# Query probabilities transposed in squares of 32 and moved within SBUF instead of by TensorE; double layer weights

## The chip, the core and the metric

The kernel runs on one NeuronCore of a Trainium2 chip. The metric is the device time of one execution in microseconds; lower is better. Five engines run their own instruction streams and meet only at semaphores: TensorE (PE, with its weight loads as PEld), VectorE (DVE), ScalarE (ACT), GpSimd (POOL) and SyncE (SP), which here only issues DMAs.

## What is computed

Eight sequences of 1024 rows by 128 columns go through a modulated layer norm, six layers of linear attention with an MLP, and a final feed-forward block with 4-bit quantisation. The change touches the attention of the six layers alone:

```python
def _linear_attn(q, k, v):
    q = jax.nn.softmax(q, axis=-1)          # over the 16 columns of a head
    k = jax.nn.softmax(k, axis=-2)          # over the 1024 rows
    context = jnp.einsum('bhnd,bhne->bhde', k, v)
    return jnp.einsum('bhnd,bhde->bhne', q, context)
...
for i in range(DEPTH):                      # 6 layers, 8 heads of 16
    xn = _layernorm(x, ln1_w[i], ln1_b[i])
    q, k, v = xn @ wq[i], xn @ wk[i], xn @ wv[i]
    x = _linear_attn(q, k, v) @ wo[i] + bo[i] + x
    xn = _layernorm(x, ln2_w[i], ln2_b[i])
    hdn = xn @ w1[i]                        # 128 -> 512
    hdn = jnp.where(hdn >= 0, hdn, LEAKY_SLOPE * hdn)
    x = hdn @ w2[i] + x
```

## The kernel before

An *item* is one sequence in one layer: `ITEMS` = 6 x 8 = 48, layer by layer, with item `i` working on sequence `i % 8`. The rows of a sequence lie on 128 partitions with T = 8 tiles of 128 columns on each, so one buffer of an item is 128 x 1024 f32. All of x stays in `x_all`.

The order of work is written out by hand. Each engine has a function `emit(v, stages)` that names its pieces of step `v` in order; step `v` works on item `v` ("ahead": norm 1, the key product), `v - 1` (attention), `v - 2` (norm 2), `v - 3` (first MLP product) and `v - 4` and `v - 5` (second MLP product and its addition). An engine never goes past a piece that waits. Buffers are single; each piece waits by semaphore for its inputs and for the readers of what it overwrites.

The pieces of an item that the texts speak of, with their lines in the program before:

- GpSimd: `root1` (L1413 to L1420) and `normalise1` (L1427, eight tiles) make `norm1`; `normalise_q` (L1461) multiplies the exponentials of q by the reciprocal sums and writes `q_prob`; `hidden_low` (L1455) is MLP work.
- TensorE: `turn_norm1` (L369) transposes `norm1` into the PSUM pair S0; `product_k` (L378) and `product_q` (L387) multiply the result, `norm1_t`, by the layer's `wk_s` and `wq_s`; `turn_k` (L393), `product_z` (L400), `turn_z` (L405), `context` (L410) and `context_out` (L415) lead to `ctx_o`, the head-masked context times `wo`; `turn_q` (L420) transposes `q_prob` into S0; `attend` (L427) multiplies `q_prob_t` by `ctx_o` into S1. `turn_norm2` is L437. `first_mlp(f, n)` (L449, L450, L453) and `second_mlp(s, t)` (L466 to L468) are eight pieces each, strewn between the others.
- ScalarE: `first_norm_t` (L628) copies S0 to `norm1_t` with the norm's weights; `exp_k` (L635), `copy_k` (L640), `exp_q` (L645); `copy_q` (L650) copies the turned `q_prob` from S0 to `q_prob_t`.
- VectorE: `max_k` (L950), `max_q` (L955), `shift_q` (L960), `sum_q` (L965), `inverse_q` (L970), `affine_z` (L987), `mask_context` (L993), `bias_context` (L999), `add_attention` (L1005, S1 added to x, signals `x_mid_ready`), the statistics of both norms (L870, L924), `add_mlp` (L1024).
- SyncE: `load_layer(l)` (L256 to L262) loads the four 128 x 128 attention weights of a layer into single buffers, each when its last reader of the layer before is through.

`product_k` of the next item writes S1, from which `add_attention` reads, and so waits for `x_mid_ready`.

## Time and profile before

| | |
|---|---|
| median of 2 runs | 1469.06 us (1468.9 to 1469.21) |
| the profiled execution: time / span | 1468.56 us / 1466.7 us |
| TensorE busy | 1294.5 us, 88% of the span |
| GpSimd busy | 1230.2 us, 84% |
| ScalarE busy | 1064.3 us, 73% |
| VectorE busy | 929.5 us, 63% |
| granted TensorE clock, mean | 0.958 of full |

The span runs from the first to the last instruction of the profiled execution; its time has 1.9 us more around it. Busy shares are averages over parts of different kinds: a start of some 120 us, the items in a fixed rhythm up to about 1140 us, and the feed-forward block after 1230 us. The clock is either at its full 2.4 GHz (1.00) or at 1.2 GHz (0.50); a number between is a mean over a stretch.

### The profile page before, as it was taken

The numbers are of one execution on the slowest core, as the hardware profiler recorded it, in microseconds if no ns is written. First come the engines' busy times: TensorE is split into PE (matmuls) and PEld (weight loads), VectorE is DVE, ScalarE is ACT, GpSimd is POOL, SyncE is SP. The second block draws the span as 40 slices with busy tenths as digits, with TensorE's granted clock in tenths as the row PEclk, the third lists the DMA queues.
The fourth block names the chain that finished last, engine by engine and source line by source line (L and its number), as shares of the span: only waits on it lengthen the run. The fifth ranks groups of instructions, "written<-read, shape, count | busy, mean of one in ns | idle before, by whom it ended". The sixth has DMA issues, their size and how long they took to land.

```text
span 1466.7 us, 31230 instructions
## 1 busy us (share of the span) xinstructions
PE 1294.5 (88%) x11006; PEld 1023.8 (70%) x11006; DVE 929.5 (63%) x2730; ACT 1064.3 (73%) x1716; POOL 1230.2 (84%) x1179
## 2 busy tenths in 40 slices
PE   5577789989999999999999999999999964788896
PEld 2455577878888788888787888887878742355564
DVE  5886645766556565565565665655655415999993
ACT  4376768778887887888878878878888854566663
POOL 4569998888988889889888898898898758999963
PEclk8789989999999999999999999999999986899999
DMA  6000000000000000000000000010000000010000
GB/s 187 15 29 15 2 1 9 2 1 2 2 8 2 2 2 2 9 2 1 2 2 9 1 2 1 2 38 2 1 2 2 2 15 29 15 44 15 29 22 38
DMA packets 12280, 20.64 MB, mean 14 GB/s; under 512 B 1024, under 2 KB 8032, under 8 KB 12128
## 3 DMA queue, kind: packets, MB, share of 16 engines
q1 hardware_dynamic: 12128, 18.65, 3.9%
q8 instruction: 91, 1.49, 0.4%
q14 instruction: 61, 0.50, 0.1%
HBM read 14.45 MB, written 4.19 MB: 13 GB/s over the span
## 4 chain that ended last, share of the span: by engine, by line
POOL 57%; issue 26%; PE 10%; DVE 4%; ACT 2%; POOLq 0%; DMA 0%; DVEq 0%; ACTq 0%
POOL hidden L1455 25%; POOL arena L1427 9%; POOL arena L1447 7%; POOL arena L1461 6%; PE ring_pair L565 1%; PE pair L587 1%; POOL arena L1554 1%; PE ring_pair L559 1%; POOL rstd L1386 1%; PE mlp L574 1%; POOL x_all L1405 1%; POOL x_all L1515 1%; POOL mod_in L1529 1%; POOL f_rstd L1386 1%; POOL ve L1434 1%
## 5 line engine op out<-in xcount | busy, mean ns | idle before, releaser
L1455 POOL TENSOR_TENSOR hidden<-hidden 128x2048 f16<-128x2048 f32 x94 | 384.4, 4089 | 14.7 <-ACT hidden L690 14.7
L683 ACT ACTIVATE hidden<-ring_pair 128x512 f32<-128x512 f32 x384 | 218.3, 591 | 64.0 <-PE ring_pair L453 57.7
L690 ACT ACTIVATE hidden<-hidden 128x2048 f16<-128x2048 f32 x96 | 183.0, 1907 | 58.1 <-PE mlp L468 58.0
L1461 POOL TENSOR_TENSOR arena<-arena,q_rec 128x1024 f32<-128x1024 f32 x48 | 97.1, 2022 | 104.8 <-DVE q_rec L970 104.8
L1386 POOL TENSOR_TENSOR rstd<-ve,minus_half 128x8 f32<-128x8 f32 x104 | 174.4, 1677 | 10.3 <-DVE ve L890 6.9
L870 DVE BATCH_NORM_STATS2 bn<-x_all 128x6 f32<-128x128 f32 x832 | 171.2, 278 | 6.1 <-DVE x_all L1005 1.4
L1427 POOL TENSOR_SCALAR arena<-x_all,rstd,nmr 128x128 f32<-128x128 f32 x384 | 167.2, 452 | 5.0
L466 PE MATMUL pair_mlp<-halves,hidden 128*128 128x128 f16 x768 | 141.9, 223 | 20.8 <-issue 14.3
L659 ACT ACTIVATE arena<-x_all,nmr,rstd 128x128 f32<-128x128 f32 x384 | 157.0, 485 | 0.0
L449 PE MATMUL ring_pair<-arena,halves 128*128 128x512 f16 x384 | 147.0, 383 | 7.4 <-ACT hidden L683 7.0
L453 PE MATMUL ring_pair<-arena,halves 128*128 128x512 f16 x384 | 146.5, 382 | 2.8 <-POOL arena L1447 2.8
L450 PE MATMUL ring_pair<-arena,halves 128*128 128x512 f16 x384 | 146.8, 382 | 0.0
L466 PE MATMUL mlp<-halves,hidden 128*128 128x128 f16 x768 | 137.2, 221 | 8.2 <-issue 8.2
L467 PE MATMUL pair_mlp<-halves,hidden 128*128 128x128 f16 x768 | 141.9, 223 | 0.0
L468 PE MATMUL pair_mlp<-halves,hidden 128*128 128x128 f16 x768 | 141.9, 223 | 0.0
L467 PE MATMUL mlp<-halves,hidden 128*128 128x128 f16 x768 | 137.2, 221 | 0.0
L468 PE MATMUL mlp<-halves,hidden 128*128 128x128 f16 x768 | 137.2, 220 | 0.0
L1447 POOL TENSOR_TENSOR arena<-arena 128x1024 f16<-128x1024 f32 x48 | 102.2, 2130 | 31.4 <-ACT arena L674 31.4
L1005 DVE TENSOR_TENSOR x_all<-pair_mlp,x_all 128x1024 f32<-128x1024 f32 x48 | 58.8, 1225 | 102.5 <-PE pair_mlp L427 102.5
L950 DVE TENSOR_REDUCE cols<-pair_mlp 128x1 f32<-128x1024 f32 x48 | 58.8, 1225 | 89.4 <-PE pair_mlp L378 89.4
L628 ACT ACTIVATE arena<-pair,ln_cols 128x1024 f32<-128x1024 f32 x48 | 57.8, 1204 | 66.8 <-PE pair L369 66.8
L427 PEld LDWEIGHTS pair_mlp<-small,arena 128*128 128x128 f32 x768 | 91.0, 195 | 18.3 <-DVE small L999 18.3
(202 smaller groups left out, 3585.5 us busy)
## 6 DMA issues: line engine op xcount, KB each, us to landing
x_in<-in_L_attn_x SPq DMA_DIRECT2D x16, 512.0 KB, 3.5
out_x<-x_all SPq DMA_DIRECT2D x8, 512.0 KB, 2.6
hidden<-in_L_attn_w SPq DMA_DIRECT2D x1, 1536.0 KB, 8.5
hidden<-in_L_attn_w SPq DMA_DIRECT2D x6, 256.0 KB, 8.1
arena<-in_L_wmod SPq DMA_DIRECT2D x1, 384.0 KB, 2.9
bo_rows<-in_L_attn_bo SPq DMA_DIRECT2D x1, 384.0 KB, 5.5
wk_s<-in_L_attn_wk SPq DMA_DIRECT2D x6, 64.0 KB, 1.8
wq_s<-in_L_attn_wq SPq DMA_DIRECT2D x6, 64.0 KB, 1.7
```

The costliest lines, as they stand in the source:

```text
L466: nc.tensor.matmul(o, rows_hi, hi, start=(c == 0), stop=False)
L467: nc.tensor.matmul(o, rows_hi, lo, start=False, stop=False)
L468: last = nc.tensor.matmul(o, rows_lo, hi, start=False, stop=(c == HC - 1))
L659: last = act.activation(tile(norm2, t), x_all[:, bass.ds((i % B) * W + t * D, D)], ACT.Identity, scale=rstd2[:, t:t + 1], bias=nmr2[:, t:t ...
L683: act.activation(hidden_t[:, c * W + h * HALF:c * W + (h + 1) * HALF], ring[n % 2], ACT.Prelu, scale=HIDDEN_DOWN, alpha=LEAKY).then_inc(hi ...
L690: act.activation(half_rows(hidden_hi, h), half_rows(hidden_t, h), ACT.Copy).then_inc(hidden_hi_ready, 1)
L870: last = nc.vector.bn_stats(bn[:, 6 * t:6 * t + 6], src(t))
L1386: return pool.tensor_tensor(rstd[:, 0:tiles], ve[:, 0:tiles], minus_half[:, 0:tiles], ALU.pow).then_inc(rstd_ready, 1)
L1427: last = pool.tensor_scalar(tile(norm1, t), x_all[:, bass.ds((i % B) * W + t * D, D)], rstd1[:, t:t + 1], nmr1[:, t:t + 1], ALU.mult, ALU.add)
L1447: pool.tensor_tensor(norm2_lo, norm2_t, norm2_hi, ALU.subtract).then_inc(norm2_lo_ready, 1)
L1455: pool.tensor_tensor(half_rows(hidden_lo, h), half_rows(hidden_t, h), half_rows(hidden_hi, h), ALU.subtract).then_inc(hidden_lo_ready, 1)
L1461: pool.tensor_tensor(q_prob.rearrange("p (g d) -> p g d", d=DH), q_exp.rearrange("p (g d) -> p g d", d=DH), q_rec[:, :].unsqueeze(2).to_br ...
```

## The change

`turn_q` on TensorE and `copy_q` on ScalarE go. In their place VectorE's `block_q` transposes `q_prob` in squares of 32 x 32 within each group of 32 partitions into a new buffer `q_blocks`, and SyncE moves the squares to their partitions in `q_prob_t` with 16 transfers for each item (`move_q`), 32 partitions x 1 KB each, written in two pieces of 512 bytes for each partition. So that the squares fall into place, `first_norm_t` writes the columns of `norm1_t` in another order, in two instructions, and `product_k` reads them back in the old order; q therefore has its rows in a permuted order until `attend`, which gives the old order again. `attend` waits for all 16 transfers, and its place on TensorE moves from ahead of `turn_norm1` to directly ahead of `product_k`; `second_mlp` 7 moves ahead of it. `turn_norm1` waits for `q_shifted` instead of `q_prob_t_ready`. The four weight buffers are doubled, so that a layer's load waits for the layer before the last.

```diff
@@ -90,7 +90,10 @@
         identity = sb("identity", P)
         head_mask = sb("head_mask", D)
         minus_half = sb("minus_half", T)
-        wk_s, wq_s, wv_s, wo_s = (sb(n, D) for n in ("wk_s", "wq_s", "wv_s", "wo_s"))
+        wk_s, wq_s, wv_s, wo_s = (sb(n, 2 * D) for n in ("wk_s", "wq_s", "wv_s", "wo_s"))
+        q_blocks = sb("q_blocks", W)[:, :]
+        QB = P // 32
+        MOVES = QB * QB
...
@@ -252,14 +255,25 @@
             sp.dma_start(bo_rows[:, :], bo_src.to_broadcast((P, DEPTH * D))).then_inc(bo_loaded, 16)
             def load_layer(l):
 
-                after(sp, k_done, l * B)
-                sp.dma_start(wk_s[:, :], wk[bass.ds(l, 1)].rearrange("l f o -> f (l o)")).then_inc(wk_ready, 16)
...
+                c = l % 2 * D
+                after(sp, k_done, (l - 1) * B)
+                sp.dma_start(wk_s[:, c:c + D], wk[l:l + 1].rearrange("l f o -> f (l o)")).then_inc(wk_ready, 16)
...
+            def move_q(i):
+
+                sp.wait_ge(q_blocks_ready, i + 1)
+                after(sp, attn_done, i)
+                for j in range(QB):
+                    to = q_prob_t[32 * j:32 * (j + 1), :].rearrange("r (a n k) -> r a n k", a=T // QB, n=QB)
+                    for n in range(QB):
+                        rows = q_blocks[32 * n:32 * (n + 1), j * T * 32:(j + 1) * T * 32].rearrange("r (a k) -> r a k", a=T // QB)
+                        sp.dma_start(to[:, :, n], rows).then_inc(q_prob_t_ready, 16)
 
             def load_x(b):
                 return sp.dma_start(x_in[:, bass.ds((b % 2) * W, W)], x_rows[bass.ds(b, 1)].rearrange("b p k -> p (b k)"))
@@ -277,14 +291,17 @@
                 sp.wait_ge(x_rest_loaded, 16 * (b - 2))
                 sp.wait_ge(front_hat_ready, b - 2)
                 load_x(b).then_inc(x_rest_loaded, 16)
-            for l in range(1, DEPTH):
-                load_layer(l)
-
-
-            sp.wait_ge(front_ready, B)
-            load_x(0).then_inc(x_back_loaded, 16)
-            sp.wait_ge(x_back_loaded, 16)
-            load_x(1).then_inc(x_back_loaded, 16)
+                move_q(b - 3)
+            load_layer(1)
+            for i in range(B - 3, ITEMS):
+                move_q(i)
+                if i == B:
+                    sp.wait_ge(front_ready, B)
+                    load_x(0).then_inc(x_back_loaded, 16)
+                    sp.wait_ge(x_back_loaded, 16)
+                    load_x(1).then_inc(x_back_loaded, 16)
+                if i % B == B - 1 and i // B + 2 < DEPTH:
+                    load_layer(i // B + 2)
 
 
             def store(b):
@@ -364,7 +381,7 @@
 
             def turn_norm1(i):
                 pe.wait_ge(norm1_ready, i + 1)
-                after(pe, q_prob_t_ready, i)
+                after(pe, q_shifted, i)
                 for t in range(T):
                     last = nc.tensor.transpose(tile(S0, t), tile(norm1, t), identity[:, :])
                 last.then_inc(t1_done, 1)
@@ -373,18 +390,20 @@
 
                 pe.wait_ge(norm1_t_ready, i + 1)
                 pe.wait_ge(wk_ready, 16 * (i // B + 1))
+                w = wk_s[:, i // B % 2 * D:i // B % 2 * D + D]
                 after(pe, x_mid_ready, i)
                 for h in range(2):
-                    last = nc.tensor.matmul(S1[:, h * HALF:(h + 1) * HALF], wk_s[:, :],
-                                            norm1_t[:, h * HALF:(h + 1) * HALF], start=True, stop=True)
+                    last = nc.tensor.matmul(S1[:, h * HALF:(h + 1) * HALF], w,
+                                            norm1_t[:, h * HALF:(h + 1) * HALF].rearrange("p (i n c) -> p n i c", i=QB, n=QB), start=True, stop=True)
                 last.then_inc(k_done, 1)
 
...
@@ -407,22 +426,18 @@
...
-
-            def turn_q(i):
-                pe.wait_ge(q_prob_ready, i + 1)
-                for t in range(T):
-                    last = nc.tensor.transpose(tile(S0, t), tile(q_prob, t), identity[:, :])
-                last.then_inc(q_turned, 1)
+                w = wo_s[:, i // B % 2 * D:i // B % 2 * D + D]
+                nc.tensor.matmul(S1[:, HALF:HALF + D], ctx_t, w, start=True, stop=True).then_inc(ctx_o_done, 1)
 
             def attend(i):
                 pe.wait_ge(ctx_o_ready, i + 1)
-                pe.wait_ge(q_prob_t_ready, i + 1)
+                pe.wait_ge(q_prob_t_ready, 16 * MOVES * (i + 1))
                 for t in range(T):
                     last = nc.tensor.matmul(tile(S1, t), tile(q_prob_t, t), ctx_o, start=True, stop=True)
                 last.then_inc(attn_done, 1)
@@ -492,17 +507,16 @@
                 if second: second_mlp(s, 4)
                 if first: first_mlp(f, 5)
                 if attention: context(a)
-                if attention: turn_q(a)
                 if first: first_mlp(f, 6)
                 if attention: context_out(a)
                 if first: first_mlp(f, 7)
-                if attention: attend(a)
                 if ahead: turn_norm1(v)
                 if norm: turn_norm2(n)
                 if second: second_mlp(s, 5)
                 if second: second_mlp(s, 6)
+                if second: second_mlp(s, 7)
+                if attention: attend(a)
                 if ahead: product_k(v)
-                if second: second_mlp(s, 7)
 
             phases(emit, pe)
             drain(emit, 0)
@@ -625,8 +639,11 @@
 
                 act.wait_ge(t1_done, i + 1)
                 after(act, q_done, i)
-                act.activation(norm1_t, S0[:, :], ACT.Identity, scale=layer_col(LN1W, i // B),
-                               bias=layer_col(LN1B, i // B)).then_inc(norm1_t_ready, 1)
+                for h in range(2):
+                    last = act.activation(norm1_t[:, h * HALF:(h + 1) * HALF].rearrange("p (i n c) -> p n i c", i=QB, n=QB),
+                                          S0[:, h * HALF:(h + 1) * HALF].rearrange("p (n i c) -> p n i c", i=QB, n=QB),
+                                          ACT.Identity, scale=layer_col(LN1W, i // B), bias=layer_col(LN1B, i // B))
+                last.then_inc(norm1_t_ready, 1)
 
             def exp_k(i):
                 act.wait_ge(k_max_ready, i + 1)
@@ -643,11 +660,6 @@
                 act.wait_ge(q_shifted, i + 1)
                 after(act, q_prob_ready, i)
                 act.activation(q_exp, q_shift, ACT.Exp).then_inc(q_exp_ready, 1)
-
-            def copy_q(i):
-                act.wait_ge(q_turned, i + 1)
-                after(act, attn_done, i)
-                act.activation(q_prob_t, S0[:, :], ACT.Copy).then_inc(q_prob_t_ready, 1)
 
             def normalise2(i, h):
 
...
@@ -968,6 +979,12 @@
                 dve.wait_ge(q_sum_ready, i + 1)
                 after(dve, q_prob_ready, i)
                 nc.vector.reciprocal(q_rec[:, :], q_sum[:, :]).then_inc(q_rec_ready, 1)
+
+            def block_q(i):
+                dve.wait_ge(q_prob_ready, i + 1)
+                after(dve, q_prob_t_ready, 16 * MOVES * i)
+                nc.vector.transpose(q_blocks.rearrange("p (j t c) -> p t j c", j=QB, t=T),
+                                    q_prob.rearrange("p (t j c) -> p t j c", j=QB, t=T)).then_inc(q_blocks_ready, 1)
 
             def inverse_k(i):
                 dve.wait_ge(k_exp_t_ready, i + 1)
@@ -1134,6 +1151,7 @@
                 if isinstance(v, int) and 4 <= v < 8:
                     prepare_gates((v - 4) // 2, v % 2 * 2 + 1)
                 if attention: affine_z(a)
+                if attention: block_q(a)
                 if isinstance(v, int) and v == 1:
                     prepare_scales()
                 if isinstance(v, int) and v == 0:
@@ -1457,7 +1475,7 @@
 
             def normalise_q(i):
                 pool.wait_ge(q_rec_ready, i + 1)
-                after(pool, q_turned, i)
+                after(pool, q_blocks_ready, i)
                 pool.tensor_tensor(q_prob.rearrange("p (g d) -> p g d", d=DH), q_exp.rearrange("p (g d) -> p g d", d=DH),
                                    q_rec[:, :].unsqueeze(2).to_broadcast((P, GROUPS, DH)), ALU.mult).then_inc(q_prob_ready, 1)
 ```

How the change moves instructions, at three places (names as in the program; `arena` holds the item buffers, `pair` is S0, `pair_mlp` is S1 and the first MLP bank, `halves` and `hidden` belong to the MLP; in brackets the semaphores waited for).

TensorE before, from `context_out` to `turn_norm2` in a step of full rhythm:

```order
L415 MATMUL pair_mlp<-wo_s,small 128x128 [waits wo_ready,ctx_t_ready]
L449 MATMUL ring_pair<-arena,halves 128x512 [waits hidden_copied,weights_ready]
L450 MATMUL ring_pair<-arena,halves 128x512
L453 MATMUL ring_pair<-arena,halves 128x512 [waits norm2_lo_ready,weights_ready]
L427 MATMUL pair_mlp<-small,arena 128x128 [waits q_prob_t_ready,ctx_o_ready]
L427 MATMUL pair_mlp<-small,arena 128x128 x7
L369 MATMUL pair<-identity,arena 128x128 [waits q_prob_t_ready,norm1_ready]
L369 MATMUL pair<-identity,arena 128x128 x7
L437 MATMUL ring_pair<-identity,arena 128x128 [waits hidden_copied,norm2_ready]
L437 MATMUL ring_pair<-identity,arena 128x128 x7
```

TensorE in the change, the same stretch (L436 is `context_out`, L386 `turn_norm1`, L452 `turn_norm2`):

```order
L436 MATMUL pair_mlp<-wo_s,small 128x128 [waits wo_ready,ctx_t_ready]
L464 MATMUL ring_pair<-arena,halves 128x512 [waits hidden_copied,weights_ready]
L465 MATMUL ring_pair<-arena,halves 128x512
L468 MATMUL ring_pair<-arena,halves 128x512 [waits norm2_lo_ready,weights_ready]
L386 MATMUL pair<-identity,arena 128x128 [waits q_shifted,norm1_ready]
L386 MATMUL pair<-identity,arena 128x128 x7
L452 MATMUL ring_pair<-identity,arena 128x128 [waits hidden_copied,norm2_ready]
L452 MATMUL ring_pair<-identity,arena 128x128 x7
```

`attend` has left this place, and the eight transposes of `turn_q`, which stood between `context` and the `first_mlp` piece ahead of `context_out`, are gone.

TensorE in the change, the end of the step and the start of the next (L483 ends `second_mlp` 7, L442 is `attend`, L396 `product_k`, L481 starts `second_mlp` 0):

```order
L483 MATMUL mlp<-halves,hidden 128x128
L442 MATMUL pair_mlp<-small,arena 128x128 [waits q_prob_t_ready,ctx_o_ready]
L442 MATMUL pair_mlp<-small,arena 128x128 x7
L396 MATMUL pair_mlp<-arena,wk_s 128x512 [waits x_mid_ready,wk_ready,norm1_t_ready]
L396 MATMUL pair_mlp<-arena,wk_s 128x512
L481 MATMUL pair_mlp<-halves,hidden 128x128 [waits x_ready,hidden_lo_ready,weights_ready]
```

`attend` now stands directly ahead of `product_k`, which waits for `x_mid_ready`; before, `turn_norm1`, `turn_norm2` and `second_mlp` 5 and 6 stood between them.

VectorE before, from `inverse_q` to `add_attention`:

```order
L970 RECIPROCAL q_rec<-q_sum 128x64 [waits q_prob_ready,q_sum_ready]
L981 TENSOR_SCALAR small<-pair_mlp,cols 128x128 [waits z_turned,k_rec_ready,z_done]
L987 TENSOR_SCALAR small<-pair_mlp,ln_cols 128x128 [waits ctx_done,z_turned]
L993 TENSOR_TENSOR small<-pair_mlp,head_mask 128x128 [waits ctx_o_done,ctx_done]
L1024 SCALAR_TENSOR_TENSOR x_all<-pair_mlp,mlp_up,x_all 128x512 [waits mlp_done]
L999 SCALAR_TENSOR_TENSOR small<-bo_rows,pair_mlp 128x128 [waits attn_done,ctx_o_done]
L1005 TENSOR_TENSOR x_all<-pair_mlp,x_all 128x1024 [waits attn_done]
```

VectorE in the change, the same stretch:

```order
L981 RECIPROCAL q_rec<-q_sum 128x64 [waits q_prob_ready,q_sum_ready]
L998 TENSOR_SCALAR small<-pair_mlp,cols 128x128 [waits z_turned,k_rec_ready,z_done]
L1004 TENSOR_SCALAR small<-pair_mlp,ln_cols 128x128 [waits ctx_done,z_turned]
L986 STREAM_TRANSPOSE q_blocks<-arena 128x8x4x32 [waits q_prob_t_ready,q_prob_ready]
L1010 TENSOR_TENSOR small<-pair_mlp,head_mask 128x128 [waits ctx_o_done,ctx_done]
L1041 SCALAR_TENSOR_TENSOR x_all<-pair_mlp,mlp_up,x_all 128x512 [waits mlp_done]
L1016 SCALAR_TENSOR_TENSOR small<-bo_rows,pair_mlp 128x128 [waits attn_done,ctx_o_done]
L1022 TENSOR_TENSOR x_all<-pair_mlp,x_all 128x1024 [waits attn_done]
```

`block_q` (L986) has come in between `affine_z` and `mask_context`; it waits for `q_prob` of GpSimd and for the transfers of the item before.

## Rows read from the trace of the kernel before

**Rows 1.** Busy time by stage (columns: stretch, us, engines, TensorE clock, DMA share, GB/s).
```profile
120.00:237.00 117.00, 94.85 (x822) 78.66 (x823) 71.18 (x215) 80.45 (x128) 106.31 (x93) 0.93 0.02 6
700.00:1140.00 440.00, 429.61 (x4073) 355.07 (x4072) 262.27 (x878) 360.13 (x513) 387.47 (x395) 1.00 0.02 5
```

**Rows 2.** Timeline of TensorE, one item (start, length, line, count, idle before).
```profile
708.22 1.95 PE L427 MATMUL pair_mlp<-small,arena 128*128 128x128 f32 x16
710.69 1.10 PE L369 MATMUL pair<-identity,arena 128*128 128x128 f32 x8 [0.52 <-POOL arena L1427]
...
713.84 1.94 PE L378 MATMUL pair_mlp<-arena,wk_s 128*128 128x512 f32 x4
715.61 0.22 PE L466 MATMUL mlp<-halves,hidden 128*128 128x128 f16 x1
...
716.95 2.00 PE L387 MATMUL pair<-wq_s,arena 128*128 128x128 f32 x16
718.79 0.22 PE L466 MATMUL pair_mlp<-halves,hidden 128*128 128x128 f16 x1
...
728.35 1.04 PE L420 MATMUL pair<-identity,arena 128*128 128x128 f32 x8
729.22 0.38 PE L449 MATMUL ring_pair<-arena,halves 128*128 128x512 f16 x1
...
733.20 1.09 PE L369 MATMUL pair<-identity,arena 128*128 128x128 f32 x8 [0.52 <-POOL arena L1427]
```

**Rows 3.** Timeline of GpSimd, same item.
```profile
725.47 1.93 POOL L1461 TENSOR_TENSOR arena<-arena,q_rec 128x1024 f32<-128x1024 f32 x1 [1.80 <-DVE q_rec L970]
...
729.70 3.45 POOL L1427 TENSOR_SCALAR arena<-x_all,rstd,nmr 128x128 f32<-128x128 f32 x8
```

**Rows 4.** Timeline of VectorE, same item.
```profile
710.21 1.23 DVE L1005 TENSOR_TENSOR x_all<-pair_mlp,x_all 128x1024 f32<-128x1024 f32 x1 [2.14 <-PE pair_mlp L427]
...
713.28 0.64 DVE L924 BATCH_NORM_AGGREGATE mv<-bn 128x2 f32<-128x6 f32 x8
...
718.99 1.22 DVE L955 TENSOR_REDUCE q_max<-pair 128x64 f32<-128x1024 f32 x1 [1.29 <-PE pair L387]
...
728.55 0.29 DVE L993 TENSOR_TENSOR small<-pair_mlp,head_mask 128x128 f32<-128x128 f32 x1 [1.77 <-PE pair_mlp L410]
```

**Rows 5.** DMA issues of the page, and SyncE's timeline.
```profile
wk_s<-in_L_attn_wk SPq DMA_DIRECT2D x6, 64.0 KB, 1.8
...
14.22 0.43 SPq L256 DMA_DIRECT2D wk_s<-in_L_attn_wk  x1
14.70 0.43 SPq L258 DMA_DIRECT2D wq_s<-in_L_attn_wq  x1
...
603.23 0.33 SPq L256 DMA_DIRECT2D wk_s<-in_L_attn_wk  x1
```

**Rows 6.** Timeline of TensorE, three gaps (last column: idle before).
```profile
154.65 0.22 PE L466 MATMUL pair_mlp<-halves,hidden 128*128 128x128 f16 x1 [3.15 <-issue]
...
183.38 0.22 PE L466 MATMUL pair_mlp<-halves,hidden 128*128 128x128 f16 x1 [3.17 <-issue]
...
212.26 0.26 PE L466 MATMUL pair_mlp<-halves,hidden 128*128 128x128 f16 x1 [3.15 <-issue]
```

**Rows 7.** Busy time and clock of stretches after the three gaps.
```profile
155.00:160.00 5.00, 5.00 (x52) 4.31 (x49) 4.78 (x9) 3.73 (x9) 4.92 (x6) 1.00 0.01 3
184.00:187.00 3.00, 3.00 (x18) 3.00 (x16) 0.00 (x0) 2.39 (x7) 3.00 (x4) 0.51 0.00 0
212.00:218.00 6.00, 5.74 (x38) 5.71 (x39) 0.75 (x1) 0.21 (x2) 5.92 (x7) 0.50 0.00 0
```

**Rows 8.** Timelines of GpSimd and VectorE at 1212 us.
```profile
1211.47 1.27 POOL L1509 TENSOR_TENSOR mod_in<-x_all,mod_out 128x512 f32<-128x512 f32 x1
1212.88 3.13 POOL L1515 TENSOR_TENSOR x_all<-mod_in,x_in 128x512 f32<-128x512 f32 x1
...
1211.99 2.89 DVE L1017 TENSOR_TENSOR hidden<-hidden 128x2048 f16<-128x2048 f32 x1
```

More of the change, by code:

```diff
@@ L385, in product_q @@
                 pe.wait_ge(wq_ready, 16 * (i // B + 1))
+                w = wq_s[:, i // B % 2 * D:i // B % 2 * D + D]
                 for t in range(T):
-                    last = nc.tensor.matmul(tile(S0, t), tile(norm1_t, t), wq_s[:, :], start=True, stop=True)
+                    last = nc.tensor.matmul(tile(S0, t), tile(norm1_t, t), w, start=True, stop=True)
                 last.then_inc(q_done, 1)
@@ L724, in emit @@
                     prepare_weights(1)
-                if attention: copy_q(a)
                 if first: hidden_high(f, 0)
```

20 lines of the change are left out of this document (10 added, 10 removed).

## Prediction

> **What bounds the kernel now.** I first read the busy time by stage [rows 1]. From 237 us on, TensorE is busy 429.6 of 440 us at the full clock (1.00) and GpSimd 387.5; between 120 and 237 us GpSimd has 106.3 of 117. Shares don't say which of the two sets the pace, so I then followed one item through the timelines of the three engines [rows 2 to 4]. `turn_norm1` (L369) starts at 710.69 and again at 733.20, so an item takes 22.51 us. The only idle time of TensorE in it is the 0.52 us ahead of L369, ended by GpSimd's L1427. The ring that closes there is:
> - `turn_norm1`, `turn_norm2`, `second_mlp` 5 and 6, from L369 to L378: 713.84 - 710.69 = 3.15
> - `product_k`, to 715.61: 1.77
> - `second_mlp` 7 and 0, to L387 at 716.95: 1.34, so 0.67 each
> - `product_q`, until VectorE's `max_q` (L955) starts at 718.99: 2.04
> - `max_q`, shift, exp, sum and reciprocal, until GpSimd's `normalise_q` (L1461) starts at 725.47: 6.48
> - `normalise_q`, `root1`, `normalise1`, until the next L369 at 733.20: 7.73
>
> The sum is 22.51, the whole period: a closed ring through TensorE, VectorE, ScalarE and GpSimd. `attend` (L427) is not in it; it fills the time in which TensorE would otherwise wait for `normalise1`. Anything put into the ring costs its full length for every item; anything taken out of TensorE elsewhere gives nothing.
>
> **The edits, one by one.** *`turn_q` and `copy_q` go.* L420 to the next L449 is 729.22 - 728.35 = 0.87 us [rows 2]. It lies between `product_q` and `turn_norm1`, where TensorE waits for GpSimd anyway; ScalarE is not late for anybody in the ring. Gain 0.
>
> *Weights double.* A load is issued in 0.33 us and lands in 1.8 [rows 5], against almost a period between the last use and the next. It was hidden, so doubling gains 0. Loads of the next layer now queue on SyncE behind the moves, with a layer to spare.
>
> *`attend` behind `second_mlp` 7, directly ahead of `product_k`.* This is the edit that counts. `product_k` waits for `x_mid_ready`, that is for `add_attention` (L1005), which waits for `attend`. Before, eight turns of norm1, eight of norm2 and two pieces of `second_mlp` covered that wait. Now the ring holds `attend` until the addition starts, 710.21 - 708.22 = 1.99 [rows 2, 4], and the addition, 1.23, with 0.05 to hand over (GpSimd's last row ends at 729.70 + 3.45 = 733.15, L369 starts at 733.20) [rows 3]. The new ring is 3.15 + 0.67 + 1.99 + 1.28 + 1.77 + 0.67 + 2.04 + 6.48 + 7.73 = 25.78, or 3.27 more. VectorE's other work doesn't lengthen it: the statistics after the addition end 713.28 + 0.64 - 710.21 = 3.71 us after its start, `max_k` (1.2) and `add_mlp` (0.7) then end about 5.6 after it, and `product_q` ends 1.28 + 1.77 + 0.67 + 2.04 = 5.76 after it. It is just covered. 40 of the 48 items lie in the stretch from 237 us on (901 us to the last `turn_norm1`): 40 x 3.27 = 131 us.
>
> *`block_q`.* The trace has no DVE transpose. The nearest rows are VectorE's passes over 128x1024 f32, 1.22 to 1.23 us [rows 4]; I take 1.2. Below it lies at best half of that, above it 2.5. It runs at 727.4, when `q_prob` is there (725.47 + 1.93), in VectorE's 1.77 us of idle time ahead of `mask_context` (L993). Queued behind it are `mask_context` and with it `context_out` on TensorE, which would be up to 1 us late at the upper end. TensorE has that time before `turn_norm1`, so it costs 0. The Trainium skill (VectorE: DVE Perf Modes, "The three transpose paths") gives 311 ns for a 128x128 bf16 transpose in squares of 32. Eight such would be an estimate of 2.5 us where my rows say 1.2; by it `q_blocks` would come 1.3 us later, and if nothing else delayed `attend`, the sum would be some 45 us higher. No row here shows which.
>
> *16 transfers on SyncE for each item.* The nearest rows are the layer loads: 0.33 us alone, 0.47 from start to start in a row of them (14.22, 14.70), 1.8 from issue to landing. I take 0.42 between issues. `q_prob` at 727.40, transpose and hand-over 1.3, 15 x 0.42 = 6.3, landing 1.8: 9.4 us. `attend` would run at 733.20 + 3.15 + 0.67 = 737.02, 9.6 us after `q_prob`. The transfers are just hidden; at 0.47 they are 0.55 us late. If a short transfer took 0.6 us to issue they would be 2.5 us late, 100 us in all.
>
> *TensorE's new idle time.* From the end of `product_q`'s issue (718.79) to `turn_norm1` stay 14.41 us, and TensorE's work in it was 11.94 (to 730.73, one period after 708.22), now 11.07 without `turn_q`. A gap of 3.3 us arises in every item ahead of `turn_norm1`, and a second one of 1.3 behind `attend`. The trace has three gaps of that size, 3.15 to 3.17 us [rows 6]. After the first the clock stayed at 1.00. Around the second it fell to its lower level, 1.2 GHz (0.51 from 184 to 187), and around the third from 212 to 218 (0.50) [rows 7]. TensorE was busy all but 0.26 us of these 9, so the losses were 0, 1.5 and 2.9 us, mean 1.5. What follows the gap here is the ring's own TensorE work, so the loss is paid in full: 40 x 1.5 = 60 us. It also delays `attend`, which hides late transfers.
>
> *First items, layer change, tail.* Between 120 and 237 us GpSimd sets the pace and TensorE has gaps of 3.15 us, just what the longer TensorE part needs: 0. The first three items have no MLP work to cover the transfers: 9.4 us instead of the 3.3 from `q_prob` (727.40) to `attend` (730.73), 6 us for each of three, of which I take 10 in all. For the last item once 4. In three items VectorE has work for the FFN weights between `max_k` and `max_q`, whose 1.29 us of slack [rows 4] is used up: 4.
>
> **Sum.** It is made against the profiled execution's 1468.56 us (median 1469.06, so 0.5 apart). 1468.6 + 131 + 10 + 4 + 4 = 1618 without the clock, and + 60 = 1678.
>
> **Rivals.** *A. Ring and clock*, 1678: the sum above. For it: two of three gaps of this size. *B. Ring alone*, 1618: the clock holds, as after the first gap. *C. Transfers late*: `attend` waits for SyncE. For it: 9.4 against 9.6 is no margin, and the gap before `attend` then adds to the idle time; with 0.55 to 2.5 us each it gives 1640 to 1720 on top of the ring, and with the clock up to 1780. Against it: a move has 64 pieces of 512 bytes, a layer load 128. *D. Not slower than before*: TensorE's own issue sets the pace, and what counts is that it loses 0.87 us of work for each item; 1468.6 - 40 x 0.87 = 1434. It decides if `normalise1` came before TensorE was through and `add_attention` cost nothing on TensorE; the 98% busy share speaks for it, against it the 0.52 us ahead of L369, ended by GpSimd each time, and the closed sum of 22.51. *E. GpSimd held up by `block_q`*: the one row of GpSimd beside a long VectorE instruction with two inputs from SBUF took 3.13 us, its neighbours of the same size 1.27 [rows 8]. If the transpose did that to `root1` and `normalise1`, the ring would grow by up to its 1.2 us, 48 in all: 1726 with the clock. The Trainium skill (SBUF — State Buffer, "Who interferes with whom") says that VectorE and GpSimd share one port pair, which a VectorE instruction takes with two SBUF inputs or in a two-port mode; the row agrees for two inputs, and the transpose has one.
>
> **How the numbers follow.** A 0.5, B 0.2, C 0.17, E 0.08, D 0.05. The likeliest gives 1678; I say 1675. The range takes in B less some microseconds and most of C: 1600 to 1765. A difference of about 2% (1440 to 1498) is what a measurement of this kernel tells from no change. D lies just at its lower edge: faster 0.03, same 0.03, slower 0.94.
>
> **What would show it.** The profile after should have: a period near 27 us from 240 us on; idle time of `product_k` ended by VectorE's addition, about 1.3 us each; idle time ahead of `turn_norm1` ended by GpSimd, about 3 us; clock below 1.00 in that stretch (B: at 1.00 and a period of 25.8); `attend` waiting for no DMA (C: it does); a transpose of 1.2 us. I am wrong if the period stays under 24 us, which would mean that the ring isn't closed as I read it, or if SyncE's 16 issues take far over 7 us.

## The result, and the profile after

The changed kernel takes 1836.5 us (median of 2 runs, 1827.74 to 1845.26) against 1469.06: a ratio of 1.250 with a 95% interval of 1.225 to 1.276, slower. The prediction said slower, but 1675 us with a range that ended at 1765. The profiled execution took 1845.26 us (span 1843.5), 377 more than that of before.

From the page of the changed kernel: busy time, the granted clock by slices, the groups of section 5 that answer to [rows 2 to 4], and the transfers.

```profile
PE 1373.4 (74%) x10622; PEld 1066.0 (58%) x10622; DVE 981.7 (53%) x2778; ACT 1033.1 (56%) x1716; POOL 1226.3 (67%) x1179
...
PEclk8689989889898989989899898989898888779999
...
L1022 DVE TENSOR_TENSOR x_all<-pair_mlp,x_all 128x1024 f32<-128x1024 f32 x48 | 58.8, 1225 | 633.5 <-PE pair_mlp L442 633.5
...
L1479 POOL TENSOR_TENSOR arena<-arena,q_rec 128x1024 f32<-128x1024 f32 x48 | 97.1, 2022 | 166.2 <-DVE q_rec L981 166.2
...
L442 PE MATMUL pair_mlp<-small,arena 128*128 128x128 f32 x768 | 116.0, 314 | 111.1 <-DMA arena<-q_blocks 111.1
...
L386 PE MATMUL pair<-identity,arena 128*128 128x128 f32 x384 | 77.2, 367 | 151.0 <-POOL arena L1445 151.0
...
L396 PE MATMUL pair_mlp<-arena,wk_s 128*128 128x512 f32 x192 | 109.2, 697 | 70.8 <-DVE x_all L1022 66.2
...
arena<-q_blocks SPq DMA_DIRECT2D x768, 32.0 KB, 1.9
```

Three waits are new in kind or size. TensorE's `product_k` (L396) now waits for VectorE's addition (L1022), 66.2 us in all; `turn_norm1` (L386) waits 151.0 us for GpSimd's `normalise1`; and `attend` (L442) waits 111.1 us for the transfers. All three are what the prediction had as signs, the third as the sign of its rival C. How they come together is seen in one item (its 16 issues hold one long one, as 22 of the 48 do): TensorE first, without the pieces of the MLP.

```profile
883.14 1.09 PE L386 MATMUL pair<-identity,arena 128*128 128x128 f32 x8 [3.16 <-POOL arena L1445]
...
890.27 2.02 PE L442 MATMUL pair_mlp<-small,arena 128*128 128x128 f32 x16 [1.51 <-DMA arena<-q_blocks]
893.70 1.96 PE L396 MATMUL pair_mlp<-arena,wk_s 128*128 128x512 f32 x4 [1.41 <-DVE x_all L1022]
...
896.16 2.00 PE L406 MATMUL pair<-wq_s,arena 128*128 128x128 f32 x16
...
912.42 1.97 PE L386 MATMUL pair<-identity,arena 128*128 128x128 f32 x8 [3.16 <-POOL arena L1445]
...
920.59 2.02 PE L442 MATMUL pair_mlp<-small,arena 128*128 128x128 f32 x16 [1.34 <-DMA arena<-q_blocks]
```

VectorE in the same item (`block_q` is L986), then GpSimd (`normalise_q` is L1479, `normalise1` L1445):

```profile
892.33 1.23 DVE L1022 TENSOR_TENSOR x_all<-pair_mlp,x_all 128x1024 f32<-128x1024 f32 x1 [12.67 <-PE pair_mlp L442]
...
898.21 1.22 DVE L966 TENSOR_REDUCE q_max<-pair 128x64 f32<-128x1024 f32 x1 [0.39 <-PE pair L406]
...
904.08 0.52 DVE L981 RECIPROCAL q_rec<-q_sum 128x64 f32<-128x64 f32 x1
...
906.65 1.25 DVE L986 STREAM_TRANSPOSE q_blocks<-arena 128x1024 f32<-128x1024 f32 x1 [0.66 <-POOL arena L1479]
907.82 0.25 DVE L1010 TENSOR_TENSOR small<-pair_mlp,head_mask 128x128 f32<-128x128 f32 x1
```

```profile
904.68 1.93 POOL L1479 TENSOR_TENSOR arena<-arena,q_rec 128x1024 f32<-128x1024 f32 x1 [2.27 <-DVE q_rec L981]
...
906.89 1.64 POOL L1404 TENSOR_TENSOR rstd<-ve,minus_half 128x8 f32<-128x8 f32 x1
...
908.91 3.45 POOL L1445 TENSOR_SCALAR arena<-x_all,rstd,nmr 128x128 f32<-128x128 f32 x8
```

And SyncE's 16 issues of the same item (the view of one line: shortest, median and longest issue in ns, the first and last start, then the time to landing):

```profile
L276 SPq DMA_DIRECT2D arena<-q_blocks x16: 586/596/1643, 907.9 to 918.5; - x16
...
DMA to landing us min/median/max: 1.9/1.9/3.1
```

Read as a ring, as [rows 2 to 4] were: `attend` at 890.27 until the addition starts 2.06, to `product_k` 1.37, to `product_q` 2.46, to `max_q` 2.05, to `normalise_q` 6.47, to `block_q` 1.97, to the first issue (907.92) 1.27, and from there to the next `attend` at 920.59 12.67. The sum is 30.32, the period of this item. The ring that closes no longer goes through `normalise1` and `turn_norm1`; it goes through SyncE: `attend` waits for the transfers in all 48 items. The 16 starts lie 0.64 us apart, here one pair 1.69, so that the last comes 10.6 us after the first. In most items without a long issue it comes 9.6 after, `attend` starts 12.9 us after `q_prob` is there, and the period is 29.3 if the clock stays up. The granted clock is below full as well:

```profile
400.00:1300.00 900.00, 699.76 (x5946) 565.76 (x5945) 424.81 (x1356) 524.92 (x765) 590.35 (x597) 0.92 0.08 20
```

The low clock costs time only where it falls between `attend` and `product_q`. That is so in 10 of the last 36 items: from `attend` to the next `normalise_q` they take 15.6 to 18.2 us, the other 26 take 14.41. In the rest the wait for the transfers covers it, as at 912.42, where `turn_norm1` takes 1.97 us instead of 1.09 and `attend` waits all the same.

### The profile page after: what moved, and what is told of

Its sections match the earlier page's. It is cut to its first block, busy times and chain, and to the rows that moved or that the text cites. A ratio compares the mean times of both kernels' runs of the same rounds, so it can differ in the third digit from the quotient of the medians.

```text
span 1843.5 us, 31325 instructions
## 1 busy us (share of the span) xinstructions
PE 1373.4 (74%) x10622; PEld 1066.0 (58%) x10622; DVE 981.7 (53%) x2778; ACT 1033.1 (56%) x1716; POOL 1226.3 (67%) x1179
## 4 chain that ended last, share of the span: by engine, by line
issue 38%; POOL 35%; PE 14%; ACT 5%; DVE 4%; SPq 3%; DMA 1%; POOLq 0%; DVEq 0%; ACTq 0%
POOL hidden L1473 10%; POOL arena L1445 7%; POOL arena L1479 5%; POOL arena L1465 5%; PE pair L386 3%; ACT arena L686 3%; SPq L276 3%; PE ring_pair L452 3%; PE pair L601 1%; PE ring_pair L579 1%; PE ring_pair L573 1%; POOL arena L1572 1%; PE pair_mlp L442 1%; PE mlp L588 1%; DVE bn L881 1%
## 5 line engine op out<-in xcount | busy, mean ns | idle before, releaser
L1022 DVE TENSOR_TENSOR x_all<-pair_mlp,x_all 128x1024 f32<-128x1024 f32 x48 | 58.8, 1225 | 633.5 <-PE pair_mlp L442 633.5
L652 ACT ACTIVATE arena<-pair_mlp,cols 128x1024 f32<-128x1024 f32 x48 | 53.5, 1114 | 363.5 <-DVE cols L961 363.5
L1479 POOL TENSOR_TENSOR arena<-arena,q_rec 128x1024 f32<-128x1024 f32 x48 | 97.1, 2022 | 166.2 <-DVE q_rec L981 166.2
L1452 POOL TENSOR_TENSOR ve<-mv,eps_cols 128x8 f32<-128x8 f32 x48 | 10.4, 218 | 286.0 <-DVE mv L935 286.0
L442 PE MATMUL pair_mlp<-small,arena 128*128 128x128 f32 x768 | 116.0, 314 | 111.1 <-DMA arena<-q_blocks 111.1
L386 PE MATMUL pair<-identity,arena 128*128 128x128 f32 x384 | 77.2, 367 | 151.0 <-POOL arena L1445 151.0
L1404 POOL TENSOR_TENSOR rstd<-ve,minus_half 128x8 f32<-128x8 f32 x104 | 171.4, 1648 | 12.2 <-DVE ve L901 8.7
L442 PEld LDWEIGHTS pair_mlp<-small,arena 128*128 128x128 f32 x768 | 106.9, 223 | 118.7 <-issue 118.7
L1445 POOL TENSOR_SCALAR arena<-x_all,rstd,nmr 128x128 f32<-128x128 f32 x384 | 167.1, 452 | 5.0
L464 PE MATMUL ring_pair<-arena,halves 128*128 128x512 f16 x384 | 147.5, 384 | 29.0 <-ACT hidden L695 28.7
L481 PE MATMUL mlp<-halves,hidden 128*128 128x128 f16 x768 | 157.3, 240 | 9.6 <-issue 9.6
L396 PE MATMUL pair_mlp<-arena,wk_s 128*128 128x512 f32 x192 | 109.2, 697 | 70.8 <-DVE x_all L1022 66.2
L386 PEld LDWEIGHTS pair<-identity,arena 128*128 128x128 f32 x384 | 60.7, 187 | 174.2 <-POOL arena L1445 174.2
L482 PE MATMUL mlp<-halves,hidden 128*128 128x128 f16 x768 | 155.9, 239 | 0.0
L483 PE MATMUL mlp<-halves,hidden 128*128 128x128 f16 x768 | 154.6, 237 | 0.0
L643 ACT ACTIVATE arena<-pair,ln_cols 128x512 f32<-128x512 f32 x96 | 69.4, 773 | 150.1 <-PE pair L386 150.1
```

The source lines that it names most:

```text
L386: last = nc.tensor.transpose(tile(S0, t), tile(norm1, t), identity[:, :])
L442: last = nc.tensor.matmul(tile(S1, t), tile(q_prob_t, t), ctx_o, start=True, stop=True)
L481: nc.tensor.matmul(o, rows_hi, hi, start=(c == 0), stop=False)
L1404: return pool.tensor_tensor(rstd[:, 0:tiles], ve[:, 0:tiles], minus_half[:, 0:tiles], ALU.pow).then_inc(rstd_ready, 1)
L1445: last = pool.tensor_scalar(tile(norm1, t), x_all[:, bass.ds((i % B) * W + t * D, D)], rstd1[:, t:t + 1], nmr1[:, t:t + 1], ALU.mult, ALU.add)
L1479: pool.tensor_tensor(q_prob.rearrange("p (g d) -> p g d", d=DH), q_exp.rearrange("p (g d) -> p g d", d=DH), q_rec[:, :].unsqueeze(2).to_br ...
```

## The experiments

All are timed beside the kernel before (its medians 1468.4 to 1469.5 us); e5 ran once, for its profile alone. To compare stretches, the starts of `add_attention` were listed from VectorE's timeline in each profile. "First 12" is the start in the 12th item, "steady" the time from there to the 48th, 36 periods (us):

| kernel | first 12 | steady | one period |
|---|---|---|---|
| before | 350.0 | 810.4 | 22.51 |
| e6, order, gap filled | 395.7 | 935.7 | 25.97 |
| e1, order alone | 401.6 | 983.5 | 26.0 or 27.6 |
| e3, change, two queues | 414.6 | 983.3 | 27.3 or 27.6 |
| after | 442.9 | 1096.4 | 29.3 to 32.5, mean 30.5 |

**The order alone.** The kernel before with only `attend` and `second_mlp` 7 in the places that the change gives them; TensorE still turns q.

```diff
-                if attention: attend(a)
...
-                if ahead: product_k(v)
                 if second: second_mlp(s, 7)
+                if attention: attend(a)
+                if ahead: product_k(v)
```

> The kernel before with one edit: attend stands behind second_mlp 7, directly ahead of product_k; turn_q and copy_q stay and nothing is transferred. Theory 1 (the ring with attend and the addition in it costs 3.3 us for each item, and the transfers the rest of what was measured): a period of 25.8 us from 240 us on, 1469 + 131 = about 1600 us, up to 1660 if the 2.4 us gap ahead of turn_norm1 lowers the clock. Theory 2 (the place of attend costs nothing, all of the loss is the transfers): 1469 us. Theory 3 (the clock is the larger part): 1700 us or more, with clock rows at 0.50 in most items.

1692.9 us (1691.1 to 1693.8), ratio 1.152 [1.150, 1.154]. Two lines of order cost 223 of the 367 us. Of 36 periods 29 are 27.6, six 26.0 and the last 26.8. In TensorE's timeline the wait for the addition is the whole of the predicted one, and the clock of the stretch is below full:

```profile
703.40 1.96 PE L378 MATMUL pair_mlp<-arena,wk_s 128*128 128x512 f32 x4 [1.41 <-DVE x_all L1005]
...
722.16 1.13 PE L369 MATMUL pair<-identity,arena 128*128 128x128 f32 x8 [2.35 <-POOL arena L1427]
```

```profile
400.00:1300.00 900.00, 776.27 (x6879) 641.26 (x6878) 440.45 (x1485) 611.61 (x859) 657.43 (x660) 0.95 0.01 4
```

**The same, with the gap filled.** In e1, sixteen identity transposes that nothing reads, ahead of `turn_norm1`. The wait for S0 to be free moves ahead of them.

```diff
+                after(pe, q_prob_t_ready, i)
+                if i > 1:
+                    for t in range(16):
+                        nc.tensor.transpose(tile(S0, t % T), identity[:, :], identity[:, :])
                 pe.wait_ge(norm1_ready, i + 1)
-                after(pe, q_prob_t_ready, i)
```

> e1_order_only with 16 transposes of the identity ahead of each turn_norm1, whose result is overwritten: work without use, 1.8 us, in the gap in which TensorE waits for normalise1. If the 1.5 us by which the long periods of e1 (27.6) stand above the short ones (26.0) are the clock falling in that gap, the clock stays at 1.00, all periods are 26.0 and the time falls by about 36 x 1.25 = 45 us to 1645, although more work is done. If the clock isn't the cause, the time stays at 1693 or rises.

```profile
400.00:1300.00 900.00, 831.80 (x7801) 693.10 (x7801) 463.00 (x1558) 639.24 (x907) 691.49 (x697) 1.00 0.01 4
```

1638.2 us (1635.9 to 1640.0), ratio 1.116 [1.113, 1.118]: more work, 55 us less time. The clock is 1.00 throughout and every period but the last 26.0. So of e1's excess the ring is 26.0 - 22.51 = 3.5 us for each item and the clock the rest, 983.5 - 935.7 = 48 us in the steady stretch, where the prediction's 1.5 for each item gives 54.

**`attend` behind two fewer pieces.** In e1, `attend` moves ahead of the last pieces, so that `second_mlp` 6 and 7 run while the addition does.

```diff
+                if attention: attend(a)
                 if second: second_mlp(s, 6)
                 if second: second_mlp(s, 7)
-                if attention: attend(a)
                 if ahead: product_k(v)
```

> e1_order_only with attend behind second_mlp 5 instead of 7, so that pieces 6 and 7 (1.34 us) cover the addition of attention ahead of product_k. By the ring it falls from 26.0 to 24.7 us, about 50 us less than e1: 1640 us. If the wait for the addition were covered by something else, 1693 us.

1609.0 us (1606.5 to 1609.8), ratio 1.095 [1.094, 1.097]. The periods are 24.6 (expected 24.7) and 26.3; the latter, where the clock fell, come in 15 of 36 items, where e1 has 29 long ones; 14 x 1.65 = 23 us of the 31 by which the time lies below what was expected. The wait for the addition is a matter of place: 1.35 us of cover gives 1.4 back.

**The shape of the transfers.** The changed kernel, with the columns of `q_prob_t` laid out so that a transfer writes 1 KB on a partition in one piece instead of two; `attend` takes its tiles in the matching order.

```diff
-                        rows = q_blocks[32 * n:32 * (n + 1), j * T * 32:(j + 1) * T * 32].rearrange("r (a k) -> r a k", a=T // QB)
-                        sp.dma_start(to[:, :, n], rows).then_inc(q_prob_t_ready, 16)
+                        rows = q_blocks[32 * n:32 * (n + 1), j * T * 32:(j + 1) * T * 32]
+                        to = q_prob_t[32 * j:32 * (j + 1), n * T * 32:(n + 1) * T * 32]
+                        sp.dma_start(to, rows).then_inc(q_prob_t_ready, 16)
```

> The change with one edit: the columns of q_prob_t are laid out so that each transfer writes 1 KB in one piece for each partition instead of two of 512 bytes; still 16 transfers of 32 KB. If the 0.64 us between two issues comes from the second dimension or the number of pieces (64 against 32), issues come every 0.33 to 0.47 us, attend no longer waits for them, and the time falls to about 1680 us. If an issue costs 0.6 us whatever the pieces, the time stays at 1836 us.

1826.1 us (1815.6 to 1834.7), ratio 1.240 [1.234, 1.247]; the median issue is 591 ns instead of 597, and 22 of the 48 bursts have one long issue, as many as before. The pieces are not the cause.

**What an issue costs.** The kernel before, with six groups of 16 issues on SyncE behind everything else, into parts of x that nobody reads any more. The first group:

```diff
+            for n in range(16):
+                sp.dma_start(x_all[32:64, n * 256:(n + 1) * 256], bo_rows[0:32, 0:256]).then_inc(priced, 16)
+            sp.wait_ge(priced, 16 * 16)
```

> The kernel before, with six groups of 16 transfers on SyncE behind the last store, each group after the landing of the one before, no engine else at work: within SBUF 32 partitions x 1 KB in one piece, then in two pieces of 512 bytes, then 128 partitions x 1 KB, then from HBM 32 partitions x 1 KB, then from HBM 128 x 1 KB, then within SBUF 16 partitions x 1 KB. They overwrite x_all when it is stored, so the output is that of before. It prices the issue. If the price hangs on the direction, the HBM groups come every 0.33 to 0.47 us and those within SBUF every 0.6; if it hangs on a queue already being full, all come alike and the first of a group is the shortest; if on the pieces, the second group is slower than the first. Total about 60 us above before.

One execution, 1536.6 us. SyncE's timeline at the end of the span (the length is that of 16 issues together):

```profile
1466.68 10.11 SPq L307 DMA_DIRECT2D x_all<-bo_rows  x16
1478.07 10.26 SPq L310 DMA_DIRECT2D x_all<-bo_rows  x16
1489.62 10.19 SPq L314 DMA_DIRECT2D x_all<-bo_rows  x16
1501.31 7.31 SPq L317 DMA_DIRECT2D x_all<-in_L_attn_x  x16
1509.91 7.55 SPq L320 DMA_DIRECT2D x_all<-in_L_attn_x  x16
1523.00 10.08 SPq L323 DMA_DIRECT2D x_all<-bo_rows  x16
```

From 32 partitions of SBUF in one piece (L307), in two pieces (L310), from 128 partitions (L314) and from 16 (L323) the 16 take 10.1 to 10.3 us, 0.63 to 0.64 each; from HBM (L317 with 32 partitions, L320 with 128) 7.3 and 7.6, 0.46 to 0.47 each. None of the 96 issues is a long one. The layer loads of [rows 5] come from HBM. They were the wrong row for a move within SBUF, and no row of before shows one. It is not the source alone: the eight stores of the kernel before (`out_x`, from SBUF to HBM, one at a time) are issued in 0.33 to 0.35 us. What makes an issue within SBUF dearer is open.

**Two queues.** The changed kernel, with ScalarE issuing half of the transfers, behind `copy_hidden` 7.

```diff
-                for j in range(QB):
+                for j in range(QB // 2):
...
+            def move_q(i):
+                act.wait_ge(q_blocks_ready, i + 1)
+                after(act, attn_done, i)
+                for j in range(QB // 2, QB):
...
+                        act.dma_start(to[:, :, n], rows).then_inc(q_prob_t_ready, 16)
...
+                if attention: move_q(a)
```

> The change with one edit: 8 of the 16 transfers are issued by ScalarE behind its last copy_hidden piece, 8 by SyncE. Theory 1 (the issues set the period): the last transfer lands 5 us earlier, attend waits only for its place behind turn_norm1, period near 25.8 us plus what the clock takes, 1620 to 1700 us. Theory 3 (clock): no more than 30 us below 1836. If it is the DMA engines and not the issuing that takes the time, also no change.

1704.0 us (1703.7 to 1705.5), ratio 1.160 [1.158, 1.161]: 132 us less than the change, and within 11 of the order alone. `attend` waits for no transfer in the steady stretch, and that stretch is as long as e1's (983.3 and 983.5). The 13 us between the two profiles are all in the first 12 items. That the two stretches are equal to 0.2 us is chance in part: e1 loses some 1.6 us to the clock in 29 of 36 items, e3 1.3 in nearly every one. But the rest of the ring is the same in both, 14.39 us from `attend` to the next `normalise_q` and 7.77 from there to `turn_norm1`. So once the transfers come in time, transposing on VectorE gives back none of what the order costs, and costs nothing beside it. The issuing was the limit, and not the DMA engines: the same 16 transfers, issued by two engines side by side (ScalarE's lie 0.66 us apart), have landed 9.2 to 10.6 us after `q_prob`, and `attend` comes after 11.0.

**Two queues, gap filled.** e3, with 24 such transposes ahead of `turn_norm1` (the diff is that of e6 with 24 for 16 and `q_shifted` for `q_prob_t_ready`).

> The kernel e3 (the change, with half of its transfers issued by ScalarE) with 24 identity transposes of 128x128 that nothing reads, ahead of turn_norm1, in the gap in which TensorE waits 3.2 us for normalise1. They add work and compute nothing. Theory: e3's period of 27.3 us is the ring of 26.0 plus what the lower clock costs, so that with the gap filled the clock stays at 1.00, the period is 26.0 and the time 1704 - 1.3 x 36 = about 1655 us. Rival: the 27.3 is something of ScalarE's or SP's issuing, and the period stays 27.3 or grows with the added work: 1704 us or more.

1667.0 us (1665.8 to 1667.6), ratio 1.135 [1.134, 1.137]. The clock is at 1.00 from 400 to 1300 us and 37 us come back of the 47 that the clock alone would give. The periods are 26.0 to 29.6, mean 26.6, since `attend` now waits for transfers again in 20 of 34 items from 400 to 1300 us, 14.2 us in all:

```profile
PE pair_mlp L445 <- DMA arena<-q_blocks: 14.2, 20, 1.9
```

This is mostly `attend` coming earlier. At the full clock it is ready 9.64 us after `q_prob`, where in e3 it was 11.0, and the last transfer has landed after 9.3 to 11.6 us, in only two of the 36 items after more than 11.0. The lower clock of e3 had covered the rest. Both theories had a part: the clock is the larger one.

**`attend` where it was.** The changed kernel, with `attend` back ahead of `turn_norm1` and `second_mlp` 7 behind `product_k`.

```diff
+                if attention: attend(a)
                 if ahead: turn_norm1(v)
...
-                if second: second_mlp(s, 7)
-                if attention: attend(a)
                 if ahead: product_k(v)
+                if second: second_mlp(s, 7)
```

> The change with attend back at its old place ahead of turn_norm1 and second_mlp 7 back behind product_k; transpose and transfers stay. Theory 1: attend waits for the transfers 13.9 us after q_prob and turn_norm1 now queues behind it, ring 1.97 + 1.27 + 12.67 + 1.74 + 3.15 + 1.77 + 1.34 + 2.04 + 6.47 = 32.4 us, so about 1900 us, slower than the change. If the new place of attend were the main cost, it would fall below 1700 us.

1998.9 us (1997.3 to 1999.5), ratio 1.360 [1.358, 1.362], period 34.1. The transfers then stand between `q_prob` and `turn_norm1`; `attend` waits 269.4 us for them in 26 items from 400 to 1300 us. The late place was thus the better one for 16 transfers, though it costs 3.5 us. The period is 1.7 above what was expected, and TensorE's timeline shows by what: behind a wait of 10.3 us `attend` takes 3.55 to `turn_norm1` at the lower clock instead of the 1.74 of the sum, and from there to `product_k` it is 4.05 instead of 3.15; against that, this item has no long issue, 1.05 less.

**Is TensorE's work worth anything?** The kernel before, with `turn_q` doing one transpose instead of eight.

```diff
-                for t in range(T):
+                for t in range(1):
                     last = nc.tensor.transpose(tile(S0, t), tile(q_prob, t), identity[:, :])
```

> The kernel before, with turn_q cut from eight transposes to one: copy_q still copies all of S0, and attend still reads all of q_prob_t, so seven eighths of the query probabilities are left untransposed. It takes 7/8 x 0.87 = 0.76 us of TensorE's work out of every item. Theory (a ring through GpSimd sets the period, and turn_q lies in TensorE's waiting time): the period stays 22.51 us and the time 1469 us. Rival D of the prediction (TensorE's own issue sets the pace): 0.76 x 40 = 30 us less, 1438 us.

1466.8 us (1465.1 to 1469.7), ratio 0.999 [0.998, 1.000]; the period stays 22.5 and TensorE waits longer instead, 38.3 us at L369 from 400 to 1100 us where it had waited 16.1. This is the change's gain on TensorE, paid out alone: nothing.

**Taking GpSimd out of the ring.** The ring of [rows 2 to 4] says what would pay: `normalise_q` stands on GpSimd ahead of `root1` and `normalise1`, 1.93 us of it. In the kernel before, it goes to VectorE.

```diff
+            def normalise_q(i):
+                dve.wait_ge(q_rec_ready, i + 1)
+                after(dve, q_turned, i)
+                nc.vector.tensor_tensor(heads(q_prob), heads(q_exp), q_rec[:, :].unsqueeze(2).to_broadcast((P, GROUPS, DH)),
+                                        ALU.mult).then_inc(q_prob_ready, 1)
...
+                if attention: normalise_q(a)
...
-                if attention: normalise_q(v - 1)
```

First directly behind `inverse_q`:

> The kernel before with one edit: normalise_q runs on VectorE behind inverse_q instead of on GpSimd. If the ring is as read, GpSimd's part of it falls by 1.93 us and root1 no longer waits for the reciprocal; the ring falls below TensorE's own 21.8 us of work, which then sets the pace: 0.7 us less for each of 40 items, about 1440 us, faster than both. If GpSimd or VectorE are held up at their shared port by it, the time is 1469 or more.

1472.4 us (1468.2 to 1474.6), ratio 1.002 [1.001, 1.004], period 22.74. TensorE's waits for GpSimd are gone, but one of another kind has come, since `scale_z` now stands behind a pass of 1.2 us:

```profile
PE pair_mlp L405 <- DVE small L987: 23.4, 31, 0.8
```

Then the same function, its call moved two pieces on, behind `affine_z`:

> The kernel before, with normalise_q moved to VectorE as in the run e7, but written behind affine_z instead of behind inverse_q. In e7 GpSimd was out of the ring and the period stayed 22.74 us, since TensorE then waited 0.8 us at turn_z for scale_z, which stood behind normalise_q. Theory (that wait was all that held e7): the period falls to TensorE's own 21.8 to 21.9 us, 0.6 x 40 = 25 us less than before, 1445 us. Rival (something of VectorE's own row, not the place of one instruction, sets the period with normalise_q there): 1469 us or more, with another wait on VectorE in each item.

1421.4 us (1421.2 to 1426.5), ratio 0.969 [0.967, 0.970], faster than both kernels. From 400 to 1100 us TensorE waits for nobody:

```profile
400.00:1100.00 700.00, 700.00 (x6720) 582.29 (x6719) 469.15 (x1482) 591.12 (x835) 601.78 (x610) 1.00 0.02 5
```

The steady stretch takes 783.8 us, 26.6 less than before (21.78 a period, as expected); another 18.4 come in the first 12 items (331.6), which I had not counted. GpSimd had set the pace in part of them and has 1.9 us less to do in each; that this is the cause was not tested.

**And `turn_q` once more,** with the same cut as in e11, now where TensorE sets the pace:

> The same cut of turn_q (one transpose instead of eight, seven eighths of the query probabilities left untransposed) in the kernel e9, in whose steady stretch TensorE waits for nobody. Theory: now TensorE's own work sets the period of 21.78 us, so the 0.76 us come off it in every item, 0.76 x 40 = 30 us, period 21.0 and 1391 us. Rival (something else stands right behind at 21.8): less than half of that, over 1406 us.

1395.6 us (1395.2 to 1400.8), ratio 0.950 [0.948, 0.952]; the period is 21.16. The cut that gave nothing before is worth 26 us here, 0.61 for each item of the 0.76 expected.

## Why the prediction was wrong

**The step that failed** is the fifth of the edits, "I take 0.42 between issues", and with it "The transfers are just hidden". The issues lie 0.64 us apart. With that the same sum, `block_q` and hand-over 1.3, issues 9.6, landing 1.9, gives 12.8 us from `q_prob` to `attend`, and 12.9 is measured in the items without a long issue; in the item shown, with one of 1.64, it is 920.59 - (904.68 + 1.93) = 13.98. Against that stand the 9.6 us of cover, which were right (9.64 in e10), so `attend` is late by 3.3 us in every item. The mechanism was named (rival C, and "if SyncE's 16 issues take far over 7 us"), but it was held for unlikely because the 0.42 came from loads out of HBM; even its upper value, 0.6 for an issue and 100 us in all, lies below what the transfers cost.

In the steady stretch of the changed kernel, from `attend` to `attend`, the ring of the new order takes 36 x (25.97 - 22.51) = 125 us more than before, the transfers 36 x (29.27 - 25.97) = 119, long issues 18, and the clock, where it falls in the ring, 23. That is 285 of 286. Without the late transfers the clock costs more: against e1, which pays 48 for it, the changed kernel is 1096.4 - 983.5 = 113 slower. In the first 12 items the transfers cost 442.9 - 401.6 = 41, where I had 10 for them.

**A second, smaller one:** "Between 120 and 237 us ... 0", and the 4 us for the FFN weights. Before any transfer is late (e1 against before) the first 12 items cost 401.6 - 350.0 = 52 us; my terms there, four periods with the clock and 4 us for the FFN weights, make 23. With the gap filled (e6) 46 remain. By periods these are 15 us in the first four, nothing in the fifth and sixth, as I had expected of all, 6 in the seventh and the eleventh, and 25 in the eighth to tenth, in which VectorE has its work for the FFN weights. Of these 25 the longer ring is 10. In each of the three, one instruction of that work takes 4.0 to 5.2 us (two of them below), 3.8 to 3.9 more than in before, 11.6 in all; that these make the remaining 15 is argued.

**What held.** The closed ring of 22.51 and the new one: 25.78 forecast, 26.0 in e1, e6 and e10. The wait of `product_k` for the addition, 1.3 forecast, 1.41 measured. The gap ahead of `turn_norm1`, 3.3 and 3.16. The transpose, 1.2 and 1.25 (L986), no sum of eight times 311 ns. Nothing for `turn_q` (e11), and nothing for `copy_q`, so far as the equal rings of e1 and e3 show it. Rival D fell with e11, and e12 shows the point from which it decides: once no ring through GpSimd stands in front. The doubled weights were not tried alone, but the last 36 periods of before are 22.50 to 22.52 us through four changes of layer, so a load that could be hidden better isn't there. Rival E fell: in 46 of the 48 items `block_q` runs beside `root1`, whose long instruction takes 1.64 us (L1404) as in before; `normalise1` takes 3.45 as in [rows 3], but it starts after `block_q` has ended and so says nothing on it.

**The clock** was the right mechanism, shown by e6, and its size fits the order alone: 54 us forecast for 36 items, 48 measured in the steady stretch. A mean over three gaps (0, 1.5 and 2.9 us) could not promise that, so the closeness is in part luck, and the prediction took gaps of 3.2 us for it where that of e1 is 2.35. In the changed kernel the clock costs 23, since the waits for transfers take its place.

The sum by differences between kernels, for the profiled executions: 1468.6, ring 125, clock 48, first 12 items 52 + 41, transfers 113, makes 1847.6; the tail gives 2 back, against 1845.3.

## What to carry to other kernels

Before moving work off an engine, find out whether its time is on the ring that closes each period: 0.76 us of TensorE's 22.51 were worth nothing until the 1.93 us of GpSimd behind them were moved, and then 0.61, and one instruction's place on VectorE then decided between 1472 and 1421 us. An engine swap that needs many small transfers is priced by issue time times count on the issuing engine, from a row of the same kind (from SBUF to SBUF, not from HBM), and both the length of the burst and the distance to its reader belong in the sum. A step directly ahead of another that waits for its consumer costs the consumer's full time; two short pieces between them give it back.

## What the runs showed of the hardware

- A DMA issue on SyncE takes 0.63 to 0.64 us from SBUF to SBUF and 0.46 to 0.47 from HBM to SBUF in a row of 16, with 32 or 128 partitions alike, and within SBUF with 16 partitions or two pieces as well (e5). Alone, a load from HBM took 0.33 and a store from SBUF to HBM 0.33 to 0.35 (before).
- In 22 of the 48 bursts of the changed kernel one issue took 1.1 to 1.8 us, all others at most 0.78. The trace's DMA records show an instruction load at each of them: a packet of 16 KB on queue q8 starts within 0.32 us of the long issue in all 22, and no other packet of q8 falls in a burst. In e2 it is again 22 of 22, and in e5 no such packet and no long issue falls in the six rows. The 18 packets of 8 KB on queue q14 that meet a burst lengthen none. Why the one kind holds an issue up is open. In the item shown, DMA from 913.4 to 913.9 us:

```profile
q1 hardware_dynamic: 73, 0.03, 25.4%
q8 instruction: 1, 0.02, 16.7%
```

- TensorE fell to its lower clock behind gaps of 2.35 us in 29 of 36 items (e1) and of 3.2 us in nearly every item (e3); useless transposes in the gap kept it at 2.4 GHz and saved 55 us (e6) and 37 us (e10).
- VectorE's TENSOR_SCALAR on 128x70 f32 took 4.04 us in e1, where in before it took 0.20, and that on 128x1120 4.66 instead of 0.78. Each started beside GpSimd's `hidden_low`; the first ended with it, the second 0.6 us after it. VectorE's and GpSimd's timelines of e1:

```profile
281.60 4.04 DVE L1181 TENSOR_SCALAR f_w_scale<-f_w_max 128x70 f32<-128x70 f32 x1
...
313.43 4.66 DVE L1189 TENSOR_SCALAR f_w_m<-f_w 128x1120 int32<-128x1120 int32 x1
```

```profile
281.51 4.08 POOL L1455 TENSOR_TENSOR hidden<-hidden 128x2048 f16<-128x2048 f32 x1
...
313.41 4.08 POOL L1455 TENSOR_TENSOR hidden<-hidden 128x2048 f16<-128x2048 f32 x1
```

The Trainium skill (SBUF — State Buffer, "Who interferes with whom") says that a VectorE instruction in a two-port mode and GpSimd exclude each other for a whole instruction; these rows agree. It also says that an instruction with one input from SBUF outside those modes doesn't contend; the transpose beside `root1`, 1.64 us with and without it, agrees.
